# A macaron attention block: a second PSUM bank for the key products, the normalized tokens one slot ahead, the next stage's tokens spread over more slots, and gate products between the last weighted values

## The reference, cut to what matters

```python
# x: 4 batches x 2048 tokens x 256, float32
x = x + 0.5 * _L0_ffn_ref(_layernorm(x, axis=-1), L0_ffn_w_gate, L0_ffn_w_up, L0_ffn_w_down)
x = x + _L0_attn_ref(_layernorm(x, axis=-1), L0_attn_Wq, L0_attn_Wk, L0_attn_Wv)
x = x + 0.5 * _L0_ffn_ref(_layernorm(x, axis=-1), L0_ffn_w_gate, L0_ffn_w_up, L0_ffn_w_down)
...
# ffn: weights (704 x 256) and activations are rounded to FP4 in blocks of 16 before each product
gate = fp4_linear(x, w_gate)
y = fp4_linear(x, w_up)
h = jax.nn.silu(gate) * y
return fp4_linear(h, w_down)
...
# attention: one head of width 256, causal, softmax(Q K^T / 16) V
scores = jnp.einsum('bqk,bsk->bqs', Q, K) * scale
weights = jax.nn.softmax(scores, axis=-1)
return jnp.einsum('bqs,bsk->bqk', weights, V)
```

## Time and profile before

| | |
|---|---|
| median of 3 runs | 1362.43 us (1360.9 to 1362.97) |
| the profiled execution's own time | 1363.96 us |
| its span, first to last instruction | 1362.2 us |
| PE busy | 1188.4 us, 87% |
| DVE busy | 1052.4 us, 77% |
| ACT busy | 733.4 us, 54% |
| POOL busy | 577.2 us, 42% |
| mean granted TensorE clock | 0.972 of full speed |

### The profile page before, as it was taken

How to read it: one execution, slowest core, us unless ns; L and a number is a source line. 1 busy time by engine, 2 the same in 40 slices (tenths; PEclk the granted TensorE clock), 3 DMA queues, 4 the chain that set the end, 5 groups by cost and what they waited for, 6 DMA issues and landing times. The chain is left out here.

```text
span 1362.2 us, 25377 instructions
## 1 busy us (share of the span) xinstructions
PE 1188.4 (87%) x7664; PEld 745.3 (55%) x7664; DVE 1052.4 (77%) x3443; ACT 733.4 (54%) x1473; POOL 577.2 (42%) x530
## 2 busy tenths in 40 slices
PE   0659999999998789989998999878999999999997
PEld 0236555555555446665665666546565555555554
DVE  5679999999999756547545654554499999999996
ACT  3456666666664444525533443545466666666652
POOL 1245554445544244434443452334344445544441
PEclk9879999999999989999999999999999999999998
DMA  9524444434444556555664656435244544545545
GB/s 319 112 51 77 87 82 81 87 75 80 87 78 78 93 100 102 102 100 88 109 118 74 104 101 120 83 62 108 50 93 102 110 100 101 110 95 107 109 100 114
DMA packets 462749, 134.46 MB, mean 99 GB/s; under 512 B 441296, under 2 KB 461904, under 8 KB 462672
## 3 DMA queue, kind: packets, MB, share of 16 engines
q1 hardware_dynamic: 454928, 125.62, 48.3%
q10 hardware_dynamic: 7744, 7.86, 1.8%
HBM read 11.34 MB, written 8.39 MB: 14 GB/s over the span
## 5 line engine op out<-in xcount | busy, mean ns | idle before, releaser
L1382 PE MATMUL ps<-wguT,arena 128*128 128x512 f16 (+1 forms) x2304 | 484.7, 365 | 28.6 <-DVE m_sb L1307 14.1
L1382 PEld LDWEIGHTS ps<-wguT,arena 128*128 128x128 f16 x2304 | 226.9, 99 | 254.7 <-issue 35.4
L516 POOL TENSOR_TENSOR arena<-arena 128x704 f32<-128x704 f32 x128 | 192.3, 1502 | 342.1 <-DVE arena L913 334.8
L1354 PE MATMUL ps<-wdT,arena 128*128 128x256 f16 x2176 | 264.1, 276 | 55.4 <-DMA arena<-arena 52.3
L1354 PEld LDWEIGHTS ps<-wdT,arena 128*128 128x128 f16 x2176 | 206.8, 99 | 119.7 <-issue 73.6
L543 POOL TENSOR_TENSOR arena<-arena 128x128 f16<-128x128 f32 (+7 forms) x64 | 143.9, 2248 | 279.0 <-ACT arena L730 231.6
L679 ACT ACTIVATE arena<-arena 128x704 int16<-128x704 f32 x128 | 100.9, 789 | 213.2 <-POOL arena L516 213.2
L1421 PE MATMUL ps<-arena 128*128 128x512 f16 (+3 forms) x960 | 194.5, 356 | 11.1 <-ACT arena L730 11.1
L1433 PE MATMUL ps<-arena 128*128 128x256 f16 x1632 | 190.4, 274 | 6.6 <-DVE x_sb L1082 6.6
L739 ACT ACTIVATE arena<-ps,arena,cst 128x128 f16<-128x128 f32 (+7 forms) x64 | 80.5, 1257 | 204.8 <-DVE arena L1071 204.8
L1433 PEld LDWEIGHTS ps<-arena 128*128 128x128 f16 x1632 | 158.9, 98 | 35.5 <-DVE x_sb L1082 8.8
(11 more groups left out here) (120 smaller groups left out, 1448.8 us busy)
## 6 DMA issues: line engine op xcount, KB each, us to landing
out_dram<-x_sb SPq DMA_DIRECT2D x32, 256.0 KB, 2.7
x_sb<-in_L_attn_x_dram ACTq DMA_DIRECT2D x3, 2048.0 KB, 17.9
arena<-arena SPq DMA_TRANSPOSE x384, 3.5
arena<-arena SPq DMA_DIRECT2D x8, 256.0 KB, 2.6
arena<-arena SPq DMA_DIRECT2D x4, 512.0 KB, 4.7
x_sb<-in_L_attn_x_dram ACTq DMA_DIRECT2D x1, 1536.0 KB, 7.6
arena<-in_L_ffn_w_down_dram SPq DMA_DIRECT2D x1, 704.0 KB, 7.8
arena<-in_L_ffn_w_gate_dram SPq DMA_DIRECT2D x1, 640.0 KB, 4.5
```

The lines of the kernel that those rows point to most:

```text
L516: g.tensor_tensor(hy[u].rearrange("p (j b) -> p b j", j=BL), h[u].rearrange("p (b j) -> p b j", j=BL), hri[u].unsqueeze(2).to_broadcast([P ...
L1354: i = nc.tensor.matmul(ps_dn[w % 2], hT[w][:, c * P:(c + 1) * P], wdT[:, k, :], start=(s == 0), stop=(s == len(DOWN_STEPS) - 1))
L1382: i = nc.tensor.matmul(psf[:, 1536 * u + lo:1536 * u + hi], xv[:, u, xl, kt, :], wguT[:, wl, lo // P:hi // P, kt, :], start=(s == 0), stop ...
```

## The change

It has four parts, and two small ones that go with them.

1. **A second bank for aux.** `aux_bank(s)` gives bank 5 (`ps_b`) to the odd slots among 0 to 7 of a batch, where scores don't use bank 5, and bank 7 to all others. In slots 1 to 8 an aux product then waits for the one before the last to be copied out (`aux_lo` at a - 1), not the last. Slot 1 also waits until the exponentials of the batch before have left bank 5.
2. **z one slot ahead.** Statistics and inverse root move to s % 4 == 3 of the group before, z and its high half to s % 4 == 0, the low half and the transposes to s % 4 == 1. The first three groups follow at the end of the first FFN: z of group 1 is transposed between the h transposes of tiles 61 and 62, z of group 0 before that of tile 60, and the statistics of group 2 are taken before the last tile's addition.
3. **x of the second FFN spread.** In the last batch ACT does mean and squares together in slot X, and x z in slot X + 1 (before: mean in X, squares and z in X + 1); POOL does the inverse root in slot X (before X + 1) and the scaling in X + 2 (before X + 3). Cells on ACT and planes on DVE stay where they were.
4. **Four tiles' gate products between the last weighted values.** Tiles 0, 1, 2 stand between weighted values 13 and 14, and tile 3 between 14 and 15 (before: 0 and 1 between 13 and 14, and 2 and 3 behind 15). The wait for the last addition (`o_add`) moves from before tile 4's gate product to before the first down product. The two last additions on DVE move two tiles back.

ACT loads its function table (Exp, later Silu) with a one-column activation of its own at the two changes of stage. At the end of the first FFN the first aux products stand one down product earlier.

```diff
+        def aux_bank(s):
+
+            return ps_b if s % TB < 2 * GT and s % 2 else ps_a
...
-                if s % GT == 2 and g % NG != 1 and g < B * NG:
+                if s % GT == 1 and g % NG != 1 and g < B * NG:
                     sp_z_T(g)
...
         def pool_slot(b, s, last=False):
-            if has_z(s, last) and s % GT == 2:
+            if has_z(s, last) and s % GT == 1:
                 pool_z_lo(b * NG + (s // GT + 2))
             if has_scores(s, last):
                 pool_p_lo(b, s)
-            if has_z(s, last) and s % GT == 0:
-                pool_z_rstd(b * NG + (s // GT + 2))
+            if has_z(s + 1, last) and s % GT == GT - 1:
+                pool_z_rstd(b * NG + ((s + 1) // GT + 2))
 
             for q in range(4):
-                if last and s == X_SLOT[q] + 1:
+                if last and s == X_SLOT[q]:
                     pool_x_rstd(NP + q, q % 2)
-                if last and q < 3 and s == X_SLOT[q] + 3:
+                if last and q < 3 and s == X_SLOT[q] + 2:
                     pool_x_y(NP + q)
...
-            if s % GT == 1 and has_z(s, last):
+            if s % GT == 0 and has_z(s, last):
                 act_z_hi(g + 2)
 
             for q in range(4):
                 if last and s == X_SLOT[q]:
                     act_x_mean(NP + q, q, q % 2)
-                if last and s == X_SLOT[q] + 1:
                     act_x_squares(NP + q, q, q % 2)
-                    if q < 3:
-                        act_x_z(NP + q, q)
+                if last and q < 3 and s == X_SLOT[q] + 1:
+                    act_x_z(NP + q, q)
...
-            if has_z(s, last):
-                if s % GT == 0:
-                    dve_z_stats(g + 2, (g + 2) * (GT * D))
-                if s % GT == 1:
-                    dve_z(g + 2, (g + 2) * (GT * D))
+            if has_z(s + 1, last) and s % GT == GT - 1:
+                dve_z_stats(g + 3, (g + 3) * (GT * D))
+            if has_z(s, last) and s % GT == 0:
+                dve_z(g + 2, (g + 2) * (GT * D))
...
-                dve_pair(first, first // 2, 0, 0, start=0, adds=((TB - 2, 1),) if first else ())
+                dve_pair(first, first // 2, 0, 0, start=0)
...
-                dve_pair(first + 1, first // 2, 1, 1, start=1, adds=((TB - 1, 0),) if first else ())
+                dve_pair(first + 1, first // 2, 1, 1, start=1, adds=((TB - 2, 0), (TB - 1, 1)) if first else ())
...
             def aux():
                 if has_next(s, last):
-                    pe_aux((g + 1) * GT + s % GT, s % GT, next_slot(s)[0])
+                    a = (g + 1) * GT + s % GT
+                    if s == 0:
+                        nc.tensor.wait_ge(res, NT)
+                    elif i == 1:
+                        nc.tensor.wait_ge(p_exp, q - 1)
+                        nc.tensor.wait_ge(aux_lo, a - 1)
+                    elif 1 <= i <= 2 * GT:
+                        nc.tensor.wait_ge(aux_lo, a - 1)
+                    else:
+                        nc.tensor.wait_ge(aux_lo, a)
+                    pe_aux(a, s % GT, next_slot(s)[0], aux_bank(s))
...
                 if s == END - 3:
                     pe.wait_ge(p_exp, NT)
-                    pe_pair(NP, NP // 2, 0, start=0)
+                    for k in range(3):
+                        pe_gate_up(NP + k // 2, NP // 2, k // 2, k % 2, k)
+                if s == END - 2:
+                    pe_gate_up(NP + 1, NP // 2, 1, 1, 3)
```

More of the change, by code:

```diff
@@ L454, in _ @@
             for k in range(NP):
-                sp_pair(k, k % 2, first=(k == 0), x2=(k < NP - 2))
-                if k == NP - 2:
-                    sp_z_T(0)
+                if k < NP - 2:
+                    sp_pair(k, k % 2, first=(k == 0))
+                else:
+                    sp_h_T(2 * k - 1, (2 * k - 1) % 4)
+                    sp_z_T(k - (NP - 2))
+                    sp_h_T(2 * k, 2 * k % 4)
             sp_h_T(NT - 1, 3)
-            sp_z_T(1)
             sp_keys_z(0)
@@ L617, in _ @@
                         pool_z_rstd(0)
-                    pool_pair(first + k, k % 2, x3=(k < NP - 3), x4=(k < NP - 4))
+                    pool_pair(first + k, k % 2, x3=(k < NP - 3), x4=(k < NP - 4), z1=(not first and k == NP - 1))
                     if not first and k == NP - 3:
@@ L685, in act_h_c, with act_pair @@
             nc.scalar.activation(hc[u], hn[u], ACT.Copy, scale=0.25 * CODE, bias=0.125 * CODE).then_inc(h_c, 1)
-        def act_pair(gp, p, odd, start=None, x2=True, x3=True, x4=True):
+        def act_pair(gp, p, odd, start=None, x2=True, x3=True, x4=True, z1=False):
             for u in range(2):
@@ L690, in act_pair @@
                 act_silu(n, u)
+                if u == 1 and z1:
+                    act_z_hi(1)
+                    act_load_table(ACT.Exp)
                 if u == 1 and x3:
@@ L821, in _ @@
                 if first:
+                    act_load_table(ACT.Silu)
                     act.wait_ge(p_lo, NT)
@@ L831, in _ @@
                 for k in range(NP - 4, NP):
-                    act_pair(first + k, k, k % 2, x2=(k < NP - 2), x3=(k < NP - 3), x4=(k < NP - 4))
+                    act_pair(first + k, k, k % 2, x2=(k < NP - 2), x3=(k < NP - 3), x4=(k < NP - 4),
+                             z1=(not first and k == NP - 1))
                     if not first and k == NP - 3:
                         act_z_hi(0)
-                if not first:
-                    act_z_hi(1)
                 n = 2 * (first + NP)
@@ L1345, in _ @@
                             dve_aux_lo(u, u, NS - 1, 0, ps_a0[u])
+                        if j == 2:
+                            dve_z_stats(2, 2 * GT * D)
         def pe_down(n, qd, w):
@@ L1356, in pe_down, with pe_gate_up @@
             i.then_inc(d_mm, 1)
+        def pe_gate_up(gp, qd, par, u, k):
+            if u == 0:
+                nc.tensor.wait_ge(x_T[par], qd * 16 + 16)
+            if k is None or k >= 2:
+                nc.tensor.wait_ge(h_h, 2 * gp + u - 1)
+            for c in range(len(GU_CUTS) - 1):
+                if k == 0 and c == 1:
+                    nc.tensor.wait_ge(w_T[1], 32)
+                i = gate_up(par, u, c)
+                if c == 1:
+                    i.then_inc(g_mm, 1)
+                if c == 2:
+                    i.then_inc(u_mm, 1)
         def pe_pair(gp, qd, par, start=None):
@@ L1360, in pe_pair @@
                 n, k = 2 * gp + u, None if start is None else 2 * start + u
-                if u == 0:
-                    nc.tensor.wait_ge(x_T[par], qd * 16 + 16)
-                if k is None or k >= 2:
-                    nc.tensor.wait_ge(h_h, n - 1)
-                for c in range(len(GU_CUTS) - 1):
-                    if k == 0 and c == 1:
-                        nc.tensor.wait_ge(w_T[1], 32)
-                    i = gate_up(par, u, c)
-                    if c == 1:
-                        i.then_inc(g_mm, 1)
-                    if c == 2:
-                        i.then_inc(u_mm, 1)
+                pe_gate_up(gp, qd, par, u, k)
+                if k == 4 and gp >= NP:
+                    nc.tensor.wait_ge(o_add, NT + 1)
                 if k is None or k >= 4:
@@ L1387, in macaron_block_kernel, with pe_aux @@
         PASSES = ((0, 0), (0, 1), (1, 0))
-        def pe_aux(a, u, slot, bank=ps_a):
+        def pe_aux(a, u, slot, bank):
             if u == 0:
                 nc.tensor.wait_ge(z_T, a * (8 * KT) + 32 * KT)
-            if not isinstance(a, int) or a > GT:
-                nc.tensor.wait_ge(aux_lo, a)
-            if isinstance(a, int) and a == GT:
-                nc.tensor.wait_ge(res, NT)
             if u < KT:
@@ L1501, in _ @@
                     continue
-                for k in range(1 if first else 0, 4):
+                for k in range(2 if first else 0, 4):
                     if not first and k == 2:
@@ L1505, in _ @@
                         pe.wait_ge(m_lo, 1)
-                    if first and k == 2:
-                        pe.wait_ge(o_add, NT + 1)
                     pe_pair(first + k, (first + k) // 2, k % 2, start=k)
@@ L1523, in _ @@
                     pe_aux(2, 2, NS - 1, ps_a0[2])
+                pe_down(n - 3, n // 4 - 1, 1)
                 pe_down(n - 2, n // 4 - 1, 2)
```

28 lines of the change are left out of this document (17 added, 11 removed).

## The result

| | before | after |
|---|---|---|
| time, median of 4 runs each | 1361.66 us (1360.48 to 1362.97) | 1326.81 us (1323.85 to 1329.21) |
| the profiled execution | 1363.96 us | 1323.85 us |
| its span | 1362.2 us | 1322.0 us |
| mean granted clock | 0.972 | 0.985 |

The ratio is 0.9744, with a 95% interval of 0.9727 to 0.9760: some 35 us were won, where 39.4 were forecast. The two profiled executions lie 40.1 us apart, more than the medians: that of the changed kernel is the fastest of its four, and that of the kernel before is slower than all four of the table.

A forecast was written before the change was run, and what follows sets the result against it. PE was taken to set the pace in attention, DVE in the second FFN. Terms 4.3 + 0 + 13.2 + 15.7 + 2.0 + 4.6 = 39.8 us off 1363.96, and 1.5 less for the median, gave 1323 us, range 1312 to 1338.

The forecast's parts named there:

- slots 16 and 17, three times: Second bank removes PE's 1.42 us wait for DVE's aux copy in slot 17, three times in the loop: 4.3 us.
- the jumps' holes and the clock behind: At the loop's jump (slot 19), the second bank wins 0: the 2.70 us hole and 1.63 us of clock stay.
- slots 4 to 8, three loop passes: z one slot ahead and second bank win 4.4 of 5.3 us in each loop pass: 13.2 us.
- last batch: In attention's last batch, 6.2 of 21.9 us of holes and clock loss are left: 15.7 us won, bounds 8 to 21.9.
- beginning of attention: Earlier z and second bank, against a wait before tile 62's down product: 2.0 us won, bounds -3 to +5.
- end of attention: From first gate to first down product, gate products cover waits and clock loss: 5.2 less 0.6, 4.6 us won.
- The 1.63 us of clock stay too: Behind the hole at the loop's jump, PE's clock loss of 1.63 us was to remain.
- the jump's hole goes: Rival: second bank or earlier fetch hides the hole at the loop's jump, 8.7 us more, 1314 us; chance 0.08.
- The second rival: ACT and DVE's chain bounds short slots and last batch (8 instead of 15.7): 17 us less, 1340 us; chance 0.12.
- Held-up softmax: Rival: z's transposes in SP's queue delay softmax transposes 11 times, up to 5.4 us each: 1383 us; chance 0.04.

The follow-up runs named there:

- bank_only: The second bank for aux alone, on the kernel before: 1354.56 us, ratio 0.9936.
- after_again: The changed kernel once more with no edit, as a measure for other runs: 1326.47 us, ratio 0.9732 to the kernel before.
- after_add_first: The changed kernel with DVE's addition ahead of z's statistics in slots 3, 7, 11 and so on: 1329.88 us, ratio 0.9774 to the kernel before.
- z_only: z one slot ahead alone, with its order around the end of the first FFN, on the kernel before: 1350.45 us, ratio 0.9904.
- x_only: x of the second FFN spread over more slots alone, on the kernel before: 1351.33 us, ratio 0.9911.
- after_z1_late: The changed kernel with z of group 1 transposed behind all h tiles: 1319.62 us, ratio 0.9706 to the kernel before.
- gate_only: Four tiles' gate products between the last weighted values alone, on the kernel before: 1357.97 us, ratio 0.9959.
- after_unrolled: The changed kernel with attention's loop of three passes written out, without jumps: 1315.15 us, ratio 0.9663 to the kernel before.
- after_one_bank: The changed kernel with the second aux bank taken back: 1332.64 us, ratio 0.9779 to the kernel before.

## Why the prediction was right, and where not

The time lies in the range and the mechanisms of the sum were there, but part of the agreement is luck. The medians give 34.9 us, 4.9 less than the sum of 39.8; the two profiled executions happen to lie 40.1 apart. And among the steps what the jumps gave beyond the forecast (3.7) stands against what slots 4 to 8 and the beginning lacked (2.8 and 2.2).

The table sets the steps of the sum against the distance between the same two instructions in the traces before and after.

| step | forecast | measured | from |
|---|---|---|---|
| slots 16 and 17, three times | 4.3 | 4.8 | 4.18 - 2.59 each time, from slot 16's aux product to slot 17's scores |
| the jumps' holes and the clock behind | 0 | 3.7 | clock 1.63 and 1.68, holes 0.61 and -0.19 |
| slots 4 to 8, three loop passes | 13.2 | 10.4 | 3.7, 4.58 - 1.63, 5.35 - 1.68 |
| last batch | 15.7 | 15.5 | 1.4 + 3.7 to slot 9, then 76.39 - 65.99 |
| beginning of attention | 2.0 | -0.2 | 44.66 to 44.84, from tile 63's gate product to slot 4 |
| end of attention | 4.6 | 5.1 | 33.41 - 28.31 |
| sum | 39.8 | 39.3 | the spans differ by 40.2 |

The slots' lines run from the aux product in slot 3 (602.66, 725.44) to that of slot 9 (638.17, 760.86 before; 628.68, 744.61 after), and in the first pass from slot 4. What is missing from the sum lies behind the first down product (1.6 us) and ahead of tile 63 (-0.8).

**The jump.** Right in its mechanism, and shown by both unrolled kernels and bank_only: the hole belongs to the jump. The Trainium skill (Runtime: NRT & Kernel Launch, section Instruction fetch mechanics) says that a taken branch to a target outside the fetched window stalls until the page has come, and that kernels prefer to be unrolled for it; the runs agree, with 1.95 to 2.94 us a jump on PE. That the fetch, and not other work of the jump, fills this time was not tested. Wrong in "The 1.63 us of clock stay too": in the changed kernel's profile and in after_again they were gone at both jumps. The rival "the jump's hole goes" fell, though a part of its gain came by way of the clock.

**Slots 4 to 8.** The mechanism was right, z's transposes ahead of time; the step that took 0.4 and 0.5 us for what was left was too small. Left were 1.93 + 0.25 + 0.87 us in pass 1 and 1.06 + 0.25 + 0.87 in pass 2. I had named slot 7's statistics as standing ahead of an addition, and not seen that slot 3's do the same to slot 4. In after_add_first the hole moved with the statistics. The second bank had no share in these slots: z_only takes 750.25 - 720.16 = 30.09 us from slot 3 to slot 9 in pass 2, the changed kernel 30.07.

**Last batch.** Right to 0.2 us, and x_only shows that the spreading of x makes it. Of the holes forecast (0.9, 0.4, 0.7, 2.1 and 0.4) there came 1.72, none, 0.60, 1.84 and 0.85: the sum of 5.0 against 4.5 is good, the split only roughly so. With x_only alone slot 12 waits 0.26 us, with all parts 1.84: once PE is faster in the slots before, it meets the chain through ACT, as forecast. The second rival wanted 7.7 us more of such waits in this batch, and they did not come.

**Beginning of attention.** The mis-sized step. Its parts were there: the hole of 4.46 us with the low clock behind it, and z of group 0 earlier. But the first scores, forecast 1 to 2 us later, came 4.5 later, and with them all that follows. z of group 2 leaves a slot earlier, but its statistics, on DVE behind tile 62's addition, start only at 469.61. SP's queue, idle from 475.71, waits 3.8 us until POOL's low half is done at 479.49; the kernel before issued the same transposes at 478.60. Counted at 482, they landed at 484.67, and PE began at 485.94, after a wait of 3.34 us, with the low clock again behind it. The timelines of SP, DVE and POOL show it:

```profile
454.43 5.13 SPq L407 DMA_TRANSPOSE arena<-arena  x4
459.66 3.15 SPq L362 DMA_TRANSPOSE arena<-arena  x2
...
469.61 1.40 DVE L1043 BATCH_NORM_STATS2 arena<-x_sb 128x6 f32<-128x256 f32 x4
...
477.37 2.12 POOL L540 TENSOR_TENSOR arena<-arena 128x1024 f16<-128x1024 f32 x1 [3.10 <-ACT arena L723]
479.51 5.16 SPq L407 DMA_TRANSPOSE arena<-arena  x4
```

Tile 62's h stands at 459.66, behind z of group 1 (454.43), which is wanted only in slot 0. after_z1_late removes just that and starts slot 4 5.3 us earlier.

**End of attention.** Right: 5.1 us for 4.6, and 5.6 us in the medians of gate_only, where the first down product waits only 0.16 us. What I took off for h's transpose (0.6) did not show: the wait is 0.17 us.

**Held-up softmax.** Its mark, weighted values that wait for DMA, appears nowhere. The changed kernel's waits of PE from 480 to 935 us, by line and releaser (us in total, times, longest), have these rows among them:

```profile
PE ps L1449 <- DVE x_sb L1096: 8.9, 13, 1.9
PE ps L1437 <- ACT arena L745: 3.5, 3, 1.8
PE ps L1415 <- DMA arena<-arena: 3.3, 1, 3.3
```

The weighted values wait for DVE's addition alone, 8.9 us in all, which is now the largest wait; DMA is left with one, that of slot 4 in the first pass.

**What stays open.** after_unrolled is 11 us below the changed kernel in the medians, where the two holes are 2.09 + 2.89 = 5.0. The traces locate 7.0: from the aux product of slot 2 to that of slot 9 the changed kernel takes 34.49 and 34.43 us in passes 1 and 2, the unrolled one 30.94 both times, 2.0 of it by smaller waits in slot 4 (0.85 for 1.93 in pass 1) and the slots behind. The rest was not located. The two profiled spans differ by only 6.3 us, for one is the fastest run of its kernel and the other the slowest of its own; against after_again it is 8.9. What decides that a hole of about 2 us is followed by the low clock was not found either, though it came far more often with one bank than with two (below).

## What to carry to other kernels

When a hole is put down to "issue", or lasts on after the work that it waited for is done, look for a jump of the loop there: here an earlier input didn't remove it, and unrolling did. When a step is moved up in a queue, name what it is moved past and when each of the two is wanted; here four transposes wanted late stood ahead of two wanted at once, which cost 5 us, because everything behind, the making of the next z too, moved with them. When PE gets faster, ask which chain it meets next, as slot 12's wait did (0.26 us alone, 1.84 with all parts). And compare the sum of a prediction with the medians, not only with the two executions that happened to be profiled.

## What the runs showed of the hardware

- At a jump of attention's loop PE stands idle for 1.95 to 2.94 us, at all twenty jumps of the ten traces that have them. With the passes written out nothing is left of it with two banks, and the 1.48 us wait for the copy with one. It is not so at every jump: in the FFN's loop, from 1000 to 1130 us of the changed kernel, PE's waits are all put down to transposes and none is over 1.0 us.
- Holes of 2 to 3 us on PE are followed by the lower level of its granted clock (1.2 GHz) in some runs and by the upper one (2.4 GHz) in others. The earlier trace rows has it behind 2.70 us; the changed kernel's profile not behind 2.09 nor 2.89, though behind its 3.34 and 4.46; after_again not behind 2.11, but behind 2.20; after_z1_late behind 1.95 and not behind 2.85. Each time the work behind it took about 1.5 to 1.7 us longer. Of the twenty jumps nine are followed by it: eight of the ten in traces with one bank (the kernel before, z_only, x_only, gate_only, after_one_bank), and one of the ten in traces with two. Why the second bank should matter is not shown. The stretch behind the 2.89 us hole in the changed kernel, and that behind the 2.20 us hole in after_again, in busy time by stretch (the share of full clock is the number ahead of the last two):

```profile
714.00:718.00 4.00, 3.46 (x24) 2.34 (x25) 1.27 (x3) 0.60 (x1) 0.00 (x0) 1.00 0.28 55
```

```profile
725.00:728.00 3.00, 3.00 (x12) 1.35 (x10) 2.90 (x11) 1.08 (x2) 1.34 (x3) 0.54 0.25 52
```

The length of a hole of this size doesn't say which of the two comes. The runs of the changed kernel lie up to 5 us apart, and the clock goes with them: in the three of nine with a mean granted clock of 0.985 or 0.986 it took 1323.85 to 1324.92 us, in the six with 0.981 or 0.982 1326.47 to 1329.21.
